# L1 attention of a transformer tower: one table set for exponential and logarithm on ScalarE, and a third query slot there

## The reference: what is computed

```
v = (x @ wqv_w.T + wqv_b).reshape(b, t, 3 * h, d)          # h = 8 heads, d = 64, t = 64 tokens
q, vf, vb = v[:, :, :h], v[:, :, h:2*h], v[:, :, 2*h:]
k = x[:, :, None, :] * wk[None, None]
a[b,s,t,h] = -sum_w |q[b,s,h,w] - k[b,t,h,w]| / sqrt(64)
a = softmax over s of (a with one more row of zeros)
bf = einsum('bsdh,bshw->bdhw', a, vf);  bb = einsum('bdsh,bshw->bdhw', a, vb)
o = (bf + bb).sum(heads);  y = o * sigmoid(1.702 * o)
x + y @ fanin_w.T + fanin_b,   on the layer-normed input, added to h
```

## Time and profile before

| | us |
|---|---|
| median of 3 runs (10531.36 to 10542.87) | 10540.28 |
| the profiled execution | 10535.12 |
| its span, first to last instruction | 10533.3 |

### The profile page before, as it was taken

The page is one execution under the profiler, slowest core; times in us unless marked ns, Lnnn a source line. Parts: engine busy times, 40 slices in busy tenths (PEclk is TensorE's granted clock), DMA queues, the critical chain, the costliest instruction groups (busy, mean ns, idle before and its releaser), DMA issues. The chain is left out here.

```text
span 10533.3 us, 156848 instructions
## 1 busy us (share of the span) xinstructions
PE 8733.2 (83%) x62276; PEld 5331.5 (51%) x62276; DVE 7088.5 (67%) x9903; ACT 4470.8 (42%) x10421; POOL 5614.7 (53%) x5677
## 2 busy tenths in 40 slices
PE   4999999999999999589688888887677588888847
PEld 2666566666666666322222222223333477777732
DVE  7999988700000788564899999993544477777753
ACT  1333433343334334233687778772333233222212
POOL 0037777777777000077555555557164377777750
PEclk7999899989999999689899999997677599999967
DMA  5000100010001000100000000000000222223220
GB/s 177 19 22 24 54 22 25 23 37 22 22 22 39 25 22 4 37 1 2 2 2 2 2 2 2 2 2 1 1 1 1 26 55 55 55 55 55 55 55 8
DMA packets 273870, 273.61 MB, mean 26 GB/s; under 512 B 204839, under 2 KB 231663, under 8 KB 267442
## 3 DMA queue, kind: packets, MB, share of 16 engines
q1 hardware_dynamic: 91602, 241.84, 6.9%
q0 software_dynamic: 181536, 21.74, 3.7%
HBM read 202.19 MB, written 60.99 MB: 25 GB/s over the span
## 5 line engine op out<-in xcount | busy, mean ns | idle before, releaser
L2453 POOL DMA_INDIRECT sorted<-by_row_rows,r_pos x2112 | 2077.3, 984 | 2571.2 <-ACT e_xt L1316 1326.4
L2570 POOL DMA_INDIRECT sorted<-r_rows,r_pos x2112 | 2082.8, 986 | 1324.3 <-DVEq L776 680.8
L2126 DVE TENSOR_TENSOR a_top<-bank,a_k 128x2048 f32<-128x2048 f32 x896 | 1972.6, 2283 | 7.9 <-ACT a_qs L2181 6.9
L2869 PE MATMUL bank<-g_tab,g_hot 128*128 128x256 f32 x6336 | 1456.6, 394 | 297.5 <-issue 181.0
L2853 POOL DMA_INDIRECT g_g<-table,g_el x1320 | 1308.7, 991 | 402.3 <-issue 402.3
L2869 PEld LDWEIGHTS bank<-g_tab,g_hot 128*128 128x128 f32 x6336 | 1250.4, 198 | 503.4 <-issue 192.9
L2328 PE MATMUL bank<-a_top,sc_pick_row 128*32 128x512 f32 x7168 | 953.8, 616 | 304.9 <-DVE a_top L2126 288.9
L2553 DVE TENSOR_TENSOR_SCAN r_work<-r_hit,r_base 128x528 f32<-128x528 bf16 (+3 forms) x900 | 1046.0, 1162 | 30.6
L816 DVE TENSOR_TENSOR f_qa<-f_qa,bank 128x512 f32<-128x512 f32 x128 | 82.3, 684 | 1442.3 <-PE bank L602 1114.2
L2174 ACT ACTIVATE a_over<-a_k,a_qs 128x64 f32<-128x64 f32 x4096 | 1021.2, 337 | 0.0
L612 PE MATMUL bank<-f_space,f_to_y 112*128 112x512 f32 x2048 | 964.5, 598 | 19.7 <-ACT f_space L704 19.7
(11 more groups left out here) (575 smaller groups left out, 13041.2 us busy)
## 6 DMA issues: line engine op xcount, KB each, us to landing
f_wm<-folded SPq DMA_DIRECT2D x16, 4608.0 KB
g_near<-near SPq DMA_DIRECT2D x198, 256.0 KB, 6.6
sorted<-r_rows,r_pos POOLq DMA_INDIRECT x2112
sorted<-by_row_rows,r_pos POOLq DMA_INDIRECT x2112, 2.1
states<-g_st SPq DMA_DIRECT2D x33, 768.0 KB, 4.0
g_g<-table,g_el POOLq DMA_INDIRECT x1320, 2.6
fp_raw<-t_modes SPq DMA_DIRECT2D x4, 2304.0 KB, 15.6
folded<-fp_turned SPq DMA_DIRECT2D x16, 576.0 KB, 9.2
```

Source lines behind the costliest of these rows:

```text
L2126: v.tensor_tensor(top[:, n % RD].rearrange("p q (h s) -> p q h s", s=S), q, kk, ALU.max).then_inc(top_done, 1)
L2453: p.indirect_dma_start(out=self.dst, out_offset=bass.IndirectOffsetOnAxis(ap=self.idx[:, k:k + 1], axis=0), in_=self.rows[:, k, :], in_off ...
L2570: p.indirect_dma_start(out=self.dst, out_offset=bass.IndirectOffsetOnAxis(ap=self.pos[:, at:at + 1], axis=0), in_=self.rows[:, part % 2, a ...
L2869: last = pe.matmul(out, hot[:, n % HB, k, j * P:(j + 1) * P], by_near[:, k, :, 0:HD * EX], start=(k == 0), stop=(k == NEAR - 1))
```

## The change

`ACT_SLOTS` goes from 2 to 3, so VectorE makes 13 tops a tile and ScalarE 12 parts. After the root and after the sigmoid ScalarE asks for the table set that holds both exponential and logarithm. The parts are spread anew over ScalarE's order, and the group work that stood after slot 13 now stands after slot 12, the last one.

```diff
-ACT_SLOTS = 2
+ACT_SLOTS = 3
...
-                        if g + 1 < GROUPS and r == 3 and i == 13:
+                        if g + 1 < GROUPS and r == 3 and i == V16 - 1:
                             scaled(g + 1)
...
-                        if g >= 1 and r == 1 and i == 13:
+                        if g >= 1 and r == 1 and i == V16 - 1:
                             add(g - 1)
...
                     act.activation(var[:], var[:], ACT.Sqrt).then_inc(std_ready, 1)
+                    act.preload_act_table_set("natural_log_exp_and_others")
...
                     act.activation(sg[:], ot[:, g % 2], ACT.Sigmoid, scale=1.702).then_inc(sg_done, 1)
+                    act.preload_act_table_set("natural_log_exp_and_others")
...
                         exp1(k - 1)
-                    over_some(k, 0, 1)
+                    over_some(k, 0, 2)
...
                         log(k - 1)
-                    over_some(k, 1, 2)
+                    over_some(k, 2, 4)
...
                         squares(g + 1)
-                    over_some(k, 2, 4)
+                    over_some(k, 4, 6)
...
                         move(k - 1)
-                    over_some(k, 4, 5)
+                    over_some(k, 6, 8)
...
                         keys(k + 1)
-                    over_some(k, 5, 6)
+                    over_some(k, 8, 9)
...
                         outs(k - 1)
-                    over_some(k, 6, 7)
+                    over_some(k, 9, 11)
...
                         hold(k + 1)
-                    over_some(k, 7, 8)
+                    over_some(k, 11, 12)
```

## The result

The changed kernel takes 10640.24 us (median of 4, 10632.03 to 10660.15) against 10536.58 us for the kernel before on the same chip: a ratio of 1.0101, 95% interval 1.0083 to 1.0118. It is slower by 104 us. The forecast was 10620, slower, in a range of 10550 to 10665.

A forecast was written before the change was run, and what follows sets the result against it. VectorE bounds the kernel's stage before, the loop through hold after: 8 x 32.30 + 2.3 + 3.8 = 264.5 us a group instead of 254.0, 84 us over eight groups, about 4 less at the ends, so +80: 10620 us, range 10550 to 10665.

The forecast's parts named there:

- The loop through the hold: From one held-queries copy to the next, over eleven tops and the out matmuls: 32.30 us, sets a tile's pace.
- VectorE's idle time: VectorE waits for held queries before each tile's first top: 3.7 us a tile, over 180 us in all.
- Table loads: ScalarE's loads in the L1 attention stage fall from 152 to about 32, sparing ScalarE 19.2 us a group.
- the group work in the loop: VectorE's work ahead of the eleventh top lengthens fourth tiles by 2.3 us and second tiles by 3.8 us a group.
- The wait for the sigmoid: In a group's second tile VectorE's gated product waits about 3.1 us for ScalarE's sigmoid.
- ScalarE's floor: ScalarE's work plus six waits for TensorE's last step: 251.6 us a group, 31.4 us a tile, under the pace.
- The loads did not stay: Rival at 5%: the common table set does not last, so loads remain and a group takes 270.9 us; 10675 us.
- ScalarE's sum: ScalarE's work in a group: 202.8 us, less 19.2 for loads, plus 61.1 for the slot: 244.6, or 30.6 a tile.
- The much faster rival: Rival at 1%: a removed load frees over twice its 1.28 us, so VectorE's 236.4 us a group sets pace; 10400 us.
- The faster case: Rival at 7%: out comes at least 0.9 us earlier, so ScalarE's work sets the pace; 10520 or 10465 us.

The follow-up runs named there:

- Hold one part earlier: Changed kernel with one ScalarE part moved from between outs and hold to ahead of outs, same instructions; 10545.9 us.
- third slot alone: Changed kernel without the two requests for the common table set, so the table loads come back; 10690.0 us.
- the last run: Changed kernel with next queries after step 8, hold ahead of outs, first part ahead of the exponential, gated after slot 7; 10487.7 us.

## Why the prediction was right

**The loop through the hold** was the right mechanism, and its size was right: 32.30 us forecast for a plain tile, 32.23 measured. That is no chance sum: in the round shown above, hold to the first top takes 0.32 us (0.36 forecast), from there to step 10 it is 24.32 (24.35), to outs 3.65 (3.65), and to the next hold 3.94 (0.12 and two parts, 3.94). Hold one part earlier undid it, while the sums of work stayed as they were.

**VectorE's idle time** was forecast at 3.7 us a tile and over 180 in all; it is 3.6 and 228.0. **Table loads** fell to 32, and the loads that left bought nothing where VectorE was the bound. A load weighs no more than its bar, as forecast: in the third slot alone the two loads of a plain tile, 2.57 us, took 1.9 us of ScalarE's waits (1.51 at outs, 0.39 in front of the logarithm) and lengthened the tile by 0.57.

**The term that was mis-sized is the group work in the loop.** It was forecast at 2.3 + 3.8 = 6.1 us a group. The wait for the sigmoid was right (3.1 forecast, 3.11 measured), but the step left out what the wait does to TensorE: idle for 4.9 us, then at half the clock, 2.1 us in the second tile, shown by keeping it busy. The fourth tile takes 34.7 to 36.3 us where 34.6 was forecast; the longest of them, too, have a slow stretch behind waits of TensorE, but that was not tested by itself. In seven groups the second tile gives 14 us and the fourth about 5, of the 22 by which the stage outran the 80 forecast.

**ScalarE's floor** of 31.4 us a tile was an average over a group, and I compared it with the loop of a plain tile. The bound of a plain tile is lower: 30.6 us in the run with hold earlier. The order of the bounds was right all the same, but in a plain tile the gap between loop and floor is 1.6 us, not the 0.9 of the forecast.

**The rivals.** The loads did not stay. ScalarE's sum was no bound in the changed kernel; it became one where the loop was shortened or the loads came back. The much faster rival asked for too much of a load: by the forecast's own sums (251.6 less 236.4 us, over 15 loads) it needs 2.3 us a load, 1.8 times the bar and not over twice; the bar of 1.28 is all that the runs show. The faster case that I had put at 7% needed the out matmuls to come earlier; the last run shows that the same end is reached by taking hold out from behind them.

## What to carry to other kernels

When work is moved from a full engine to one with room, add up not only the engines but every loop of waits that crosses them: here hold, eleven tops, a step, the out matmuls, outs and a few parts, 30.39 us hidden under 30.8 before and 32.30 after. Look in such a loop for a small copy that releases the next round and stands late in its engine's order; moving it ahead costs no work. And if a wait is added for TensorE, look at the granted clock behind it: here 4.9 us of idle time cost another 2.1 us in the matmuls that followed.

## What was not expected of the hardware

An idle stretch of 4.9 us of TensorE cost more than itself: the next 8.6 us ran at a granted clock of 0.50, and four matmuls that nothing reads gave 2.1 us a group back. The profile can put a wait down to "issue" though a semaphore ends it: VectorE's 206.6 us under that name are the wait for hold, as the 0.09 us between hold's end and the top's start show.
